# One core, a feed-forward, attention, feed-forward layer: rows of attention's third and fourth blocks transposed by DMA instead of by the tensor engine

## The reference, cut to what matters

```python
x = x + 0.5 * ffn(layernorm(x))      # ffn: silu(x @ Wg) * (x @ Wu) @ Wd, weights packed in 4 bits
x = x + attention(layernorm(x))      # 2 sequences of 1024 rows, one head of width 128
x = x + 0.5 * ffn(layernorm(x))      # x: [2, 1024, 512] float32

def attention(x):
    qkv = x @ Wqkv + bqkv            # [.., 512] @ [512, 3 * 128]
    p = softmax(q @ k.T / sqrt(128))
    return (p @ v) @ Wo + bo         # back to 512 columns
```

## Time and profile before

| what | value |
|---|---|
| median of 3 runs | 825.32 us (824.76 to 825.58) |
| the profiled execution, its time / its span | 824.82 us / 822.9 us |
| PE busy | 98% of the span |
| DVE / ACT / POOL busy | 60% / 33% / 33% |
| DMA | 151.43 MB, mean 184 GB/s |

### The profile page before, as it was taken

How to read it: one execution, slowest core, us unless ns; L and a number is a source line. 1 busy time by engine, 2 the same in 40 slices (tenths; PEclk the granted TensorE clock), 3 DMA queues, 4 the chain that set the end, 5 groups by cost and what they waited for, 6 DMA issues and landing times. The chain is left out here.

```text
span 822.9 us, 10477 instructions
## 1 busy us (share of the span) xinstructions
PE 809.3 (98%) x3868; PEld 665.1 (81%) x3868; DVE 494.3 (60%) x809; ACT 272.5 (33%) x469; POOL 271.8 (33%) x219
## 2 busy tenths in 40 slices
PE   5999999999999999999999999999999999999998
PEld 4877778878888888788898888888878788888786
DVE  7889945756654543557766896546347743443452
ACT  3433433555211211343656872121123321211221
POOL 6646614651115363203064371064431110110100
PEclk9999999999999999999999999999999999999999
DMA  6899958965754467344053159644767164444131
GB/s 168 261 342 288 325 188 278 348 261 231 266 188 160 135 205 201 102 153 154 1 176 131 40 179 356 232 145 159 233 188 225 52 213 159 133 168 133 29 104 52
DMA packets 92221, 151.43 MB, mean 184 GB/s; under 512 B 42860, under 2 KB 53796, under 8 KB 87178
## 3 DMA queue, kind: packets, MB, share of 16 engines
q1 hardware_dynamic: 85492, 139.36, 50.8%
q10 hardware_dynamic: 5814, 7.17, 2.5%
q0 software_dynamic: 864, 4.23, 2.0%
HBM read 104.30 MB, written 42.17 MB: 178 GB/s over the span
## 5 line engine op out<-in xcount | busy, mean ns | idle before, releaser
L868 PE MATMUL ps<-blk,ring 128*128 128x512 f32 (+1 forms) x1386 | 320.8, 389 | 0.0
L868 PEld LDWEIGHTS ps<-blk,ring 128*128 128x128 f32 (+1 forms) x1386 | 256.7, 185 | 57.9 <-POOL blk L2290 0.3
L875 PE MATMUL ps<-wd,hT 128*128 128x512 f32 (+1 forms) x1056 | 250.8, 391 | 0.4 <-DVE hT L1775 0.3
L875 PEld LDWEIGHTS ps<-wd,hT 128*128 128x128 f32 (+1 forms) x1056 | 197.3, 188 | 43.1 <-DVE hT L1775 0.8
L2355 POOL TENSOR_TENSOR h<-h,u 128x512 f32<-128x512 f32 (+1 forms) x33 | 42.7, 1294 | 300.1 <-ACT h L1505 300.1
L875 PE MATMUL ps<-xT,wp 128*128 128x512 f32 x480 | 114.3, 394 | 0.1
L875 PEld LDWEIGHTS ps<-xT,wp 128*128 128x128 f32 x480 | 91.0, 190 | 20.0 <-issue 0.7
L1778 DVE TENSOR_TENSOR u<-ps,p1s 128x512 f32<-128x512 f32 (+1 forms) x66 | 45.3, 687 | 95.7 <-PE ps L868 95.7
L1505 ACT ACTIVATE h<-h 128x512 f32<-128x512 f32 (+1 forms) x33 | 20.9, 632 | 176.9 <-DVE h L1778 176.9
L1778 DVE TENSOR_TENSOR h<-ps,p1s 128x512 f32<-128x512 f32 (+1 forms) x33 | 22.8, 690 | 63.9 <-PE ps L868 63.9
L1778 DVE TENSOR_TENSOR u<-ps,u 128x512 f32<-128x512 f32 (+1 forms) x66 | 45.6, 691 | 24.6 <-PE ps L868 23.5
(11 more groups left out here) (142 smaller groups left out, 897.5 us busy)
## 6 DMA issues: line engine op xcount, KB each, us to landing
ring<-wsaved SPq DMA_DIRECT2D x29, 1024.0 KB, 5.2
ring<-wsaved SPq DMA_DIRECT2D x33, 768.0 KB, 4.6
wsaved<-wp SPq DMA_DIRECT2D x10, 1024.0 KB, 4.9
stream<-xres SPq DMA_DIRECT2D x32, 256.0 KB, 2.3
xn<-stream SPq DMA_DIRECT2D x8, 1024.0 KB, 6.8
xres<-stream SPq DMA_DIRECT2D x32, 256.0 KB, 3.2
wfull<-wf ACTq DMA_DIRECT2D x20, 256.0 KB, 5.6
wsaved<-wp SPq DMA_DIRECT2D x10, 512.0 KB, 5.1
```

The source lines that it names most:

```text
L868: mm = pe.matmul(ps[0:w, bank, :], ring[:, slot, which, a, kt, 0:w], blk[:, which, b, kt, :], start=not onto and kt == 0 and n == 0, stop= ...
L875: mm = pe.matmul(bank_ap, lhs(a), rhs(b), start=first and n == 0, stop=last and n == 2)
```

## The change

`PLANED` gets blocks 6 and 7. PE no longer transposes them. DVE no longer normalises them: POOL does, tile by tile, with the pulling apart of the halves (`normalise`), block 6 ahead of the first `add_bias` and block 7 ahead of the first `total`. The mean and variance of block 6 are taken earlier (beside the down projection of the first feed-forward, after lows 7 and 8), and the high and low parts of blocks 4 and 5 are made earlier there too. `t_hi` and `t_lo` of blocks 6 and 7 now read SBUF (`xn`), not PSUM; those of block 6 stand later on ACT and DVE. Every DMA transpose, of all six planed blocks, is issued as four, one a k-tile; those of block 7 stand in two places of SP's list. Three waits of SP that counted PE's transposes count low parts instead.

```diff
-PLANED = (4, 5, 10, 11)
+PLANED = (4, 5, 6, 7, 10, 11)
...
-            def turn_planes(t):
+            def turn_planes(t, kts=range(KT)):
                 sp.wait_ge(*planes_stored(t))
-                sp.dma_start_transpose(xn[:, t % 2, :, :].bitcast(U16), planes[t].rearrange("n h c -> (n h) c")).then_inc(d_xT[t % 2], 16)
+                for k in kts:
+                    sp.dma_start_transpose(turned_rows(t, k).bitcast(U16),
+                                           planes[t].rearrange("n h c -> (n h) c")[:, k * P:(k + 1) * P]).then_inc(d_xT[t % 2], 16)
...
             store_rows(3, stream, SEQ + ROWS)
+            store_planes(6)
...
                     load_rows(7, stream, SEQ + ROWS)
+                    turn_planes(6)
+                    store_planes(7)
+                    turn_planes(7, (0, 1))
                 else:
-                    sp.wait_ge(s_turn, ROWS_TURNED)
+                    sp.wait_ge(s_alo, 4 * KT)
                     load_rows(9, stream, TOKENS + ROWS)
...
                     load_residual(k + 1, stream, base + ROWS, [j - 1])
+                    if b == 0 and j > 1:
+                        turn_planes(7, [j])
...
-                if a:
-                    pe.wait_ge(s_out, QT)
-                    turn(4 + a + 1, (2, 3))
                 turn_v(a)
...
-                pe.wait_ge(s_ln[t + 1], RT)
-                turn(t + 1, range(KT))
                 pe.wait_ge(s_qkvlo, 3 * a + 1)
                 score(b, 0)
                 score(b, 1)
...
                 project(b, QT - 2)
-                pe.wait_ge(s_ln[7], RT)
-                turn(7, (0, 1))
                 qkv_product(2, 0, (2, 3))
...
             for b in range(2):
-                a, t = 2 * b, 6 + 2 * b
-                ln_stats(t)
-                ln_var(t)
+                a = 2 * b
+                if b:
+                    ln_stats(8)
+                    ln_var(8)
                 qk_lo(a, 0, qT)
-                if b == 0:
-                    ln_apply(t)
-                else:
-                    ln_shift(t)
+                if b:
+                    ln_shift(8)
...
-                t_lo(2, range(KT))
                 maximum(b, 0)
                 maximum(b, 1)
                 ln_stats(t)
                 p_lo(b, 0)
+                ln_var(t)
...
-                    if g == 3:
-                        ln_apply(t, (0, 1, 2))
+                    if g in (1, 2):
+                        t_lo(2, (2 * g - 2, 2 * g - 1))
                     heads_out(b, g)
-                    if g == 3:
-                        ln_apply(t, (3,))
                 t_lo(3, (0, 1))
...
+            def normalise(t):
+                for r in range(RT):
+                    ln_apply(t, [r])
+                    to_planes(t, [r])
...
                 deviation(6 + 2 * b)
+                if b == 0:
+                    normalise(6)
                 add_bias(b, range(RT))
                 deviation(7 + 2 * b)
                 if b:
                     ln_apply(9, (0, 1))
+                else:
+                    normalise(7)
```

More of the change, by code:

```diff
@@ L325, in macaron @@
             sem(n) for n in ("s_silu", "s_rhi", "s_whi", "s_th13", "s_th24", "s_p1", "s_g1", "s_g2", "s_hhi", "s_x21", "s_xhi", "s_shi"))
-        s_ahi, s_qhi, s_qkvhi, s_exp, s_phi, s_ohi, s_out, s_planes = (
-            sem(n) for n in ("s_ahi", "s_qhi", "s_qkvhi", "s_exp", "s_phi", "s_ohi", "s_out", "s_planes"))
+        s_ahi, s_qhi, s_qkvhi, s_exp, s_phi, s_ohi, s_out = (
+            sem(n) for n in ("s_ahi", "s_qhi", "s_qkvhi", "s_exp", "s_phi", "s_ohi", "s_out"))
+        s_planes = [sem(f"s_planes{n}") for n in range(2)]
         s_unp, s_int, s_wf, s_tab, s_oh, s_h, s_rlo, s_t13, s_tlo13 = (
@@ L375, in hidden @@
             return h2_back[:, NT - 1 - i, :]
-        ROWS_TURNED = 6 * KT
+        ROWS_TURNED = 4 * KT
         def turned(q, what, kt):
@@ L891, in turn_block @@
                 turn_tile(turn_at(q, what, kt), t, kt + (2 if what in (A12, A22) else 0))
-            def turn(t, kts):
-                for k in kts:
-                    turn_tile(TURN_BANK[k], t, k)
             def down(q, half, i, rows=range(RT)):
@@ L1208, in qkv_second @@
                     score(b, 1)
+                    pe.wait_ge(s_out, QT)
                     qkv_product(a, 0, (0, 1, 2))
@@ L1552, in bottom @@
                             copy(wo[:, 0, :], wo_raw[:, :]).then_inc(s_qhi, 1)
-                        if i in (first + 2, second + 2):
-                            t_hi((i - first - 2) // 2, range(KT))
+                        if i in (3, 4):
+                            t_hi(i - 3, range(KT))
                         continue
@@ L1574, in t_hi @@
                 for k in kts:
-                    if a < 2:
-                        act.wait_ge(*planes_turned(4 + a))
-                        src = turned_rows(4 + a, k)
-                    else:
-                        act.wait_ge(s_turn, 16 + KT * (a - 2) + k + 1)
-                        src = ps[:, TURN_BANK[k], :]
-                    copy(x_turned(a)[:, 0, k, :], src).then_inc(s_ahi, 1)
+                    act.wait_ge(*planes_turned(4 + a))
+                    if a >= 2:
+                        act.wait_ge(s_qkv, 3 * (a - 1))
+                    copy(x_turned(a)[:, 0, k, :], turned_rows(4 + a, k)).then_inc(s_ahi, 1)
             for r in range(RT):
@@ L1733, in _ @@
                     break
-                t_hi(2, range(KT))
                 exp(b, 0)
@@ L1741, in _ @@
                 v_hi(a)
+                t_hi(2, range(KT))
                 for g in range(QT // 2):
@@ L1803, in ln_shift @@
                                          in1=rstd[:, t % 2, first:end], op0=ALU.mult, op1=ALU.mult).then_inc(s_nmr, 1)
[L1805 to L1810, removed]
             def x_sum(q, what, kt):
@@ L2056, in bottom @@
                     if q == 1:
-                        if i in (first + 2, second + 2):
-                            t_lo((i - first - 2) // 2, range(KT))
+                        if i in (3, 4):
+                            t_lo(i - 3, range(KT))
+                        if i in (7, 8):
+                            ln_stats(6, (0, 1) if i == 7 else (2, 3))
+                        if i == 8:
+                            ln_var(6)
                         continue
@@ L2080, in t_lo @@
                     dve.wait_ge(s_ahi, KT * a + k + 1)
-                    src = turned_rows(4 + a, k) if a < 2 else ps[:, TURN_BANK[k], :]
-                    minus(dst[:, 1, k, :], src, f32(dst[:, 0, k, :])).then_inc(s_alo, 1)
+                    minus(dst[:, 1, k, :], turned_rows(4 + a, k), f32(dst[:, 0, k, :])).then_inc(s_alo, 1)
             tables = maker(dve, s_tab)
```

19 lines of the change are left out of this document (7 added, 12 removed).

## The result

The changed kernel took 829.12 us (median of 5 runs, 828.58 to 830.78). The kernel before took 825.24 (5 runs, 824.67 to 825.58) on the same chip. The ratio is 1.0052, 95% interval 1.0039 to 1.0066. The forecast was 827.9, with a range of 823.4 to 830.0. The profiled execution took 829.1, of which 827.3 us are the span; before, the span was 822.9.

A forecast was written before the change was run, and what follows sets the result against it. PE, busy 98% of the span, was taken as the bound: -3.5 (transposes) + 1.7 (K's low part) + 1.75 (block 7's third low part) + 2.6 (third and fourth later) = +2.6, so 827.9 us; range 823.4 to 830.0.

The forecast's parts named there:

- Removed work: PE's 16 transposes each of blocks 6 and 7 go, 0.109 us apiece, 3.5 us in all.
- First place: Ahead of the scores behind K of block 5: PE waits 1.7 us for K's low part; 0.03 comes back.
- Second place, start of the chain: K of block 7: earlier PE gains nothing; low part 1 ends 0.8 us late and moves DVE's chain to low part 3.
- the two lockouts: POOL's total blocks low part 1 (0.8 us late); its biases block low parts 3 and 4 (1.55 and 2.7 late).
- The sum: Whole kernel: -3.5 + 1.7 + 1.75 + 2.6 = +2.6 us, 827.9 on the median.
- Behind it PE has no spare time in which to catch up: After block 7's fourth k-tile of K, the rest of PE's list moves by 2.6 us.
- the forecast case: Block 7's low parts locked out by POOL: +1.9 to +3.0 us with biases starting between 440.7 and 441.6; chance 0.52.
- late transfers: Rival: SP pieces cost over 2.5 us each or block 7 lands after 394; 829 to 835 us, chance 0.10.
- the fall as a rival of its own: PE's clock: about 4 us of work behind the second wait at half pace, 2 us more, 830; chance 0.07.
- The covers: POOL's normalising and SP's transposes and loads for blocks 6 to 8 stay hidden, covered by 1.5 to 3 us.
- A piece on SP: Each quarter DMA transpose takes SP 1.03 to 1.48 us, upper bound 5.9.

The follow-up runs named there:

- 2: Changed kernel with POOL's sequence 1 biases held until block 7's fourth low part and its seventh query tile's total until the second; 824.64 us, 0.9991 of the kernel before.
- 4: Changed kernel with 16 unused dummy transposes put where block 6's stood, ahead of the first scores; 829.20 us, 1.0043 of the kernel before.
- experiment 1: Changed kernel with POOL's biases of sequence 1 held until block 7's fourth low part; 825.86 us, 1.0007 of the kernel before.
- experiment 3: Changed kernel with PE's two waits in K of block 7 filled with unused transposes (26 and 6); 826.73 us, 1.0013 of the kernel before.
- experiment 5: Changed kernel with block 7's high and low parts 3 and 4 made directly behind 1 and 2; 826.99 us, 1.0020 of the kernel before.
- 7: Changed kernel with three of four k-tiles of V of block 5 put ahead of the first scores; 828.20 us, 1.0040 of the kernel before.
- 9: Changed kernel with block 7's low parts 3 and 4 behind 1 and 2, POOL's seventh total held for all four, `nmr` later; 824.35 us, 0.9990 of the kernel before.
- 6: Changed kernel with block 7's low parts 3 and 4 early and block 8's mean and variance later on DVE; 829.04 us, 1.0046 of the kernel before.
- 11: Changed kernel with DMA transposes issued whole again, except block 7's four pieces; 829.00 us, 1.0049 of the kernel before.
- 8: Changed kernel with V of block 5 ahead of first scores, block 7's low parts early, block 8's statistics later; 828.19 us, 1.0037 of the kernel before.
- 12: Changed kernel with V ahead of first scores, block 7's low parts early, total held, `nmr` later, block 9's load before residuals; 822.79 us, 0.9968 of the kernel before.

## Why the prediction was right, and the term it left out

- **Removed work.** 32 transposes at 0.109 us: right, and worth nothing to the scores by themselves (experiments 2 and 4).
- **First place.** Forecast: 1.7 us of waiting for K's low part, 0.03 back. Measured: 1.56 on the wait, and 4.61 became 4.58.
- **Second place, start of the chain.** The low parts were forecast 0.8 late at the first, the biases at 441.05, low part 3 done at 442.9 and 4 at 444.65, PE's third tile at 442.95 and the fourth at 444.7. Measured, with 0.63 taken off: biases 441.07, third tile 442.93, fourth 444.62. Experiments 1 and 2 took the two lockouts away one at a time and gave back what each was said to cost. The rule of the Trainium skill, page "SBUF — State Buffer", section "SBUF: two separate sides", was that the loser is fully blocked for a whole instruction; this trace agrees, with 1.39 and 1.77 us for subtractions of 0.68.
- **The sum.** Forecast +2.6, of which the measured fourth tile bears out 2.5. The step that failed is the one after: "Behind it PE has no spare time in which to catch up; the rest of the list moves by 2.6". It moved by 4.1 to the scores (66.10 - 61.99), since the clock fell behind the two waits (1.6 to 1.7 us, experiment 3), and 0.34 was caught up by the last projection (111.48 - 107.71 = 3.77). So the measured +3.9 lies above the +1.9 to +3.0 of the forecast case. It is inside the range only because the top, 830.0, left room for the clock and for late transfers; this much was luck, while the path up to the fourth tile was not. The prediction had the fall as a rival of its own at 0.07, priced at 2 us and 830 in all. It was no rival but a consequence of the forecast, and belonged into its sum at a fair chance: the wait of 3.3 us was worked out, and only the question of what PE does behind it was left to the side. The prediction also read the earlier trace rows as a full clock throughout; a row of nines says 90% or more in each 20.6 us, and the changed kernel prints the same row over a fall of 3.4 us. The page "TensorE: Matmul & The Clock Gate" of the Trainium skill, section "HAM oscillation — how this bites in real kernels", warned of it; experiment 3 shows it here.
- **The covers.** POOL normalised block 6 from 366.82 to 379.8 (forecast 366 to 380) and block 7 from 398.87 (398.3); block 8's load went out at 427.55 (427 or 428). All were hidden, as forecast. A piece on SP was taken as 1.03 to 1.48 us; the row says 1.16 to 4.71 (ns on SP, min/median/max):

```profile
L640 SPq DMA_TRANSPOSE xn<-planes x24: 1159/1301/4711, 306.7 to 631.6; - x24
...
DMA to landing us min/median/max: 3.4/3.9/7.8
```

The long ones stand behind the load of block 7, where nobody waited for them.

What stays open: why a wait of 2.4 us in experiment 1 seems to be followed by the lower clock in some executions and not in others (in experiment 5, with 2.35, all eleven have a mean clock of 0.998 or less), and what besides the clock spreads the executions of experiments 7 and 9. Both would take a profile of more than one execution of a kernel.

## What to carry to other kernels

Before you take work off the bound engine, ask what the next instruction on it waits for, and when that is ready: removed work that ends at the same moment as someone's low part was only filling a wait, and the gain comes when other work of the same list is put there. When an operand moves from PSUM to SBUF, look for POOL instructions beside every VectorE operation that now has two SBUF sources, the tiny ones too. And a wait that you have worked out is not the end of the sum: price PE's clock behind it, and on the other engines whoever is queued behind a late instruction, not only who reads its result.

## What the runs showed of the hardware that I had not expected

- PE's granted clock in the profiles: behind waits of 1.56 us at the first place (the change, 1 to 3, 5, 6, 9, 11) and 1.64 at the second (2) it stayed full; behind 2.35 (experiment 5), 2.38 (1), 2.39 (7), 2.95 to 3.10 followed by 0.72 or 0.73 (the change, 4, 11) and 4.6 (6, 8) it fell to 1.2 GHz for the work that followed, which cost 1.6 to 1.7 us where it was isolated (3, 5). The fall is not at one distance from the wait: in 7 the clock was 0.50 in the microsecond in which PE went on (440 to 441), in the change it was still full for 1.7 us behind the longer wait.
- A VectorE instruction of 0.16 us (`nmr`, 128x4) took 1.24 us beside POOL's biases, as much as one of POOL's instructions lasts.
- The start of the program moves attention by up to 2.4 us from one execution to the next (383.37 to 385.76), more than most edits here are worth; it is there already at 62 us (61.63 in 2, 64.08 in 12 for the same matmul). Distances between two points of one trace are free of it. They are still those of one execution, as 3 and 7 show, where a race between a low part and a bias fell out well by itself.
